# Wide attention products written as four 32-column products, one per column group of TensorE

## The reference

```python
q1 = _split_heads(x @ Wq1, H); q2 = _split_heads(x @ Wq2, H)      # H = 16, head width d = 32
k = _split_heads(x @ Wk, H);   v = _split_heads(x @ Wv, H)
q = jnp.concatenate([q1, q2], axis=1)
k2 = jnp.repeat(k, 2, axis=1); v2 = jnp.repeat(v, 2, axis=1)
scores = jnp.einsum('bhqd,bhkd->bhqk', q, k2) * scale
scores = jnp.where(causal, scores, jnp.finfo(scores.dtype).min)
p = jax.nn.softmax(scores, axis=-1)
y = jnp.einsum('bhqk,bhkd->bhqd', p, v2)
y1, y2 = (y[:, :H], y[:, H:])
y = y1 - lam * y2                                                 # lam = sigmoid(x @ Wlam)
return y.reshape(B, T, D) @ Wo
```

## Time and profile before

| | |
|---|---|
| median of 3 runs | 2073.38 us |
| profiled execution | 2072.73 us |
| its span | 2070.8 us |
| TensorE matmul, share of the span | 96% |
| VectorE, ScalarE, GpSimd | 64%, 40%, 43% |
| mean granted TensorE clock | 0.992 |

### The profile page before, as it was taken

The page is one execution under the profiler, slowest core; times in us unless marked ns, Lnnn a source line. Parts: engine busy times, 40 slices in busy tenths (PEclk is TensorE's granted clock), DMA queues, the critical chain, the costliest instruction groups (busy, mean ns, idle before and its releaser), DMA issues.

```text
span 2070.8 us, 29135 instructions
## 1 busy us (share of the span) xinstructions
PE 1987.4 (96%) x11271; PEld 870.9 (42%) x11312; DVE 1330.7 (64%) x2622; ACT 827.8 (40%) x1259; POOL 880.4 (43%) x459
## 2 busy tenths in 40 slices
PE   7898999899999998999999999999999879899999
PEld 3444444444444444343433434343433324444444
DVE  5868686747847545566666666666667754775644
ACT  4435343425444412344443433344434442543431
POOL 3757575700000000666666667776776670000000
PEclk9999999999999999999999999999999999999999
DMA  7101010120000020000101010010000201000001
GB/s 239 36 26 36 31 36 31 60 94 1 1 0 1 0 57 18 22 16 21 21 22 21 12 28 10 21 22 21 1 22 6 83 10 41 1 0 22 21 1 41
DMA packets 71562, 59.72 MB, mean 29 GB/s; under 512 B 37312, under 2 KB 55744, under 8 KB 71168
## 3 DMA queue, kind: packets, MB, share of 16 engines
q1 hardware_dynamic: 64512, 45.27, 7.6%
q10 hardware_dynamic: 6912, 12.59, 1.9%
HBM read 43.02 MB, written 10.62 MB: 26 GB/s over the span
## 4 chain that ended last, share of the span: by engine, by line
PE 53%; DVE 5%; POOL 2%; ACT 1%; issue 1%; DMA 0%; DVEq 0%; SPq 0%; POOLq 0%; ACTq 0%
PE psum L128 9%; PE psum L1217 9%; PE psum L1308 8%; PE psum L1363 6%; PE psum L1346 6%; PE psum L152 5%; PE psum L1255 3%; PE psum L1342 2%; POOL b_totals L1592 2%; PE psum L1320 2%; PE psum L1265 1%; PE psum L1333 1%; DVE psum L1659 1%; DVE b_maxima L1664 1%; DVE b_down L1722 0%
## 5 line engine op out<-in xcount | busy, mean ns | idle before, releaser
L1592 POOL TENSOR_TENSOR b_totals<-b_totals,b_probs 128x2048 f32<-128x2048 f32 (+5 forms) x160 | 504.4, 3152 | 271.6 <-ACT b_probs L1508 265.8
L1659 DVE CUSTOM_DVE_ANT_0 psum<-psum,b_rest 128x384 f32<-128x384 f32 (+3 forms) x512 | 236.1, 522 | 206.8 <-PE psum L1308 206.6
L1508 ACT ACTIVATE b_probs<-psum 128x1024 f32<-128x1024 f32 (+3 forms) x320 | 228.6, 765 | 244.5 <-PE psum L1346 229.2
L447 PE MATMUL psum<-hT,a_win 128*128 128x512 f32 x640 | 292.5, 600 | 2.6 <-DVE a_parts L751 1.2
L128 PE MATMUL psum<-hT,b_early 128*128 128x512 f16 x1024 | 228.2, 382 | 9.8 <-DVE b_middle L214 6.9
L128 PE MATMUL psum<-hT,W 128*128 128x512 f16 x1024 | 227.4, 382 | 3.7 <-DVE a_win L214 3.6
L1664 DVE TENSOR_REDUCE b_maxima<-psum 128x2 f32<-128x1024 f32 x128 | 150.8, 1220 | 105.9 <-PE psum L1308 105.9
L447 PEld LDWEIGHTS psum<-hT,a_win 128*128 128x128 f32 x640 | 120.2, 192 | 130.5 <-issue 129.2
L128 PEld LDWEIGHTS psum<-hT,b_early 128*128 128x128 bf16 x1024 | 100.1, 98 | 135.2 <-issue 9.7
L128 PEld LDWEIGHTS psum<-hT,W 128*128 128x128 bf16 x1024 | 100.7, 99 | 126.2 <-issue 6.8
L1564 POOL MEMSET b_mask<- 128x128 f32 x1 | 0.2, 204 | 352.2 <-POOLq L279 352.2
(11 more groups left out here) (232 smaller groups left out, 3291.2 us busy)
## 6 DMA issues: line engine op xcount, KB each, us to landing
a_parts<-in_w_guT ACTq DMA_DIRECT2D x32, 256.0 KB, 2.8
ternary<-W SPq DMA_DIRECT2D x1, 6144.0 KB, 18.3
a_win<-in_w_inT SPq DMA_DIRECT2D x20, 256.0 KB, 7.8
a_parts<-in_w_pT ACTq DMA_DIRECT2D x16, 256.0 KB, 2.6
b_down<-lam_rows SPq DMA_DIRECT2D x32, 128.0 KB, 2.6
b_early<-ternary SPq DMA_DIRECT2D x8, 512.0 KB, 8.1
out<-x SPq DMA_DIRECT2D x16, 256.0 KB, 2.2
x<-in_x SPq DMA_DIRECT2D x3, 1024.0 KB, 8.0
```

Source lines behind the costliest of these rows:

```text
L447: last = pe.matmul(ring(s, j), win[:, at:at + P], core["hT"][:, (i * KT + k) * BLK:(i * KT + k + 1) * BLK], start=(k == 0), stop=(k == KT ...
L1508: act.activation(held(u, s)[:, 2 * a:2 * a + 2, off:BLK], pair_banks(("score", u, s, a))[:, :, off:BLK], ACT.Exp, scale=SCALE).then_inc(ex ...
L1592: pool.tensor_tensor(acc, acc, held(u, s)[:, own, off:BLK], ALU.add).then_inc(summed, 1)
L1659: last = dve.tensor_tensor_reduce(scores, scores, row_mask[:, BLK - width:BLK], 1.0, -3e38, ALU.add, ALU.max, maxima[u % 2][:, at:at + 1])
```

## The change

Every product with 128 output partitions in the five places named is written as four products with 32 output partitions each. The four have the same moving operand and each has a quarter of the stationary one; the sums and the place of the results in PSUM stay the same. Semaphore waits stand ahead of the first of the four, and the signal is on the last.

```diff
 HEAD_AT = [0, 2, 1, 3]
+COLUMNS = [slice(j * HD, (j + 1) * HD) for j in range(HPT)]
@@ project (keys, queries)
-                return pe.matmul(to, weights[:, k * P:(k + 1) * P], hT[:, at:at + BLK],
-                                 start=(k == 0), stop=(k == KT - 1))
+                for own in COLUMNS:
+                    last = pe.matmul(to[own, :], weights[:, k * P + own.start:k * P + own.stop], hT[:, at:at + BLK],
+                                     start=(k == 0), stop=(k == KT - 1))
+                return last
@@ fill, values
-                        last = pe.matmul(to[:, t % 2 * 2 * P:(t % 2 + 1) * 2 * P], hT[:, at:at + P],
-                                         wv_all[:, k * D + h * P:k * D + (h + 2) * P],
-                                         start=(k == 0), stop=(k == KT - 1))
+                        for own in COLUMNS:
+                            last = pe.matmul(to[own, t % 2 * 2 * P:(t % 2 + 1) * 2 * P],
+                                             hT[:, at + own.start:at + own.stop],
+                                             wv_all[:, k * D + h * P:k * D + (h + 2) * P],
+                                             start=(k == 0), stop=(k == KT - 1))
@@ output
-                    last = pe.matmul(to[:, j], yT[r % 2][:, t * P:(t + 1) * P], wo_sl[r % 2][:, :],
-                                     start=True, stop=True)
+                    for own in COLUMNS:
+                        last = pe.matmul(to[own, j], yT[r % 2][:, t * P + own.start:t * P + own.stop],
+                                         wo_sl[r % 2][:, :], start=True, stop=True)
@@ scores, mask
-                        pe.matmul(to[j // 2][:, j % 2, off:off + P], ident_b[:, :], later_key[:, :],
-                                  start=True, stop=True)
+                        for own in COLUMNS:
+                            pe.matmul(to[j // 2][own, j % 2, off:off + P], ident_b[:, own], later_key[:, :],
+                                      start=True, stop=True)
```

## The result

The changed kernel takes 2063.03 us (median of 4 runs, 2059.48 to 2063.65) against 2073.40 for the kernel before (4 runs, 2073.01 to 2074.82): a ratio of 0.9946, with a 95% interval from 0.9934 to 0.9958. The forecast was 2062.

The account below looks back on a forecast made before the run. TensorE's own sequence was taken to bound attention. Terms 7.8 + 4.9 + 2.3 − 1.1 − 0.3 − 0.2 − 1.0 − 1.0 = 11.4 us off 2072.73 gave 2061.3, with 0.65 for the median 2062 us; range 2057 to 2084.

Parts of the forecast that it names:

- the issue rival: Issue of four times the instructions becomes TensorE's bound: 2081 us at 33 ns each with half the lookahead; chance 0.16.
- (a): Runs of projections, values or outputs behind another shape, with any mask right behind: 130, each 0.06 cheaper, 7.8 us saved.
- (b): Projection between `weigh` and `row` (steps 0 and 4): 27 places, each 0.18 cheaper, 4.9 us saved.
- (c): `den` (15) or `weigh` (6) right ahead of a mask: a 0.11 change of shape gone, 2.3 us saved.
- the gain goes into waits: Rival: TensorE's gain is lost waiting for the exponential and the maximum in most steps, 2071 us; chance 0.12.
- (d): Behind the still wide `neg` (16 places): 0.16 lost each, counted as 1.1 us for outputs and 0.3 for masks.
- (e): Mask: sixteen narrow bf16 products take what four took; 0.2 us lost where it follows `row` alone.
- (f): Steps 4 and 5: scores wait for the row scores' maximum, so a shorter fill gains nothing; 1.0 us lost.
- (g): Issue of four times the matmul instructions, where a semaphore lets the queue start afresh: 1 us charged.

Follow-up runs that it names:

- e1: The kernel before with only the mask products in 32 columns: 2081.89 us, ratio 1.0040.
- e2: The changed kernel with the mask products wide again, all else narrow: 2072.40 us, ratio 0.9994.
- e3: The kernel before with only the projection between `weigh` and `row` (steps 0 and 4) written in four: 2067.23 us, ratio 0.9972.
- e7: The changed kernel with two products of 64 columns in place of four of 32: 2066.89 us, ratio 0.9967.
- e5: The changed kernel with the last feed-forward layer's up products (f16) in four as well: 2066.55 us, ratio 0.9965.
- e8: The changed kernel with each narrow mask product cut in four along its moving columns, results not the same, read for time alone: 2096.06 us, one run.
- e4: The changed kernel with the output or mask right behind `neg` kept in one wide product: 2064.40 us, ratio 0.9955.

## Why the prediction was right

The theory: what is saved is a gap between groups of different shapes, in which the array is emptied, and the wait for a run's first weights, which is as long as the columns of the load. The rival: four times as many instructions cost issue time. e1 and e2 (parts that don't add), e3 (one join by itself), e7 (a join lost by another width) and e5 (27 ns an instruction held) bear out the first, as far as gap and wait go; that the array is being emptied in the gap is a name for it that no run shows. e8 shows that the issue rival, which lost from 31 ns an instruction on, has no place here.

Point by point, by the starts of all places of a kind before and after:

- (a), 130 runs: forecast 0.06 each, measured 0.060 (a run into scores, 35 places, 0.060; a run into a mask 0.080, less 0.020 for the mask).
- (b), 27 joins with `weigh`: forecast 0.18, measured 0.197 (0.113 ahead of the projection, 0.084 behind); by e3 0.19.
- (c), 21 joins of `den` or `weigh` with a mask: forecast 0.11, measured 0.116. Behind 1578 us, in the last units, it does not last: there TensorE stops in the middle of many masks for ScalarE's exponential, which does not come sooner. The mask that follows `weigh` at 1688.98 us, for instance, waited 1.68 us before its second half, and 1.88 now. What the joins and runs gain in that stretch, about 1.0 us, goes into such waits: the rival "the gain goes into waits", true in this one place.
- (d), behind `neg`: mis-sized. Forecast 0.16 each and 1.4 us in all; the output or mask starts 0.095 later, and e4 shows that none of it reaches the turn. What failed is the step "VectorE's addition too": that the addition ends later because the output does. VectorE isn't waiting for the output there. From the end of `row` on it goes through the maxima, their rounding and that of `neg` without an idle moment, and starts the addition when that is done. In the changed kernel:

```profile
1147.71 0.30 DVE L1666 CUSTOM_DVE_ANT_0 psum<-psum,b_rest 128x128 f32<-128x128 f32 x1 [0.80 <-PE psum L1313]
...
1149.71 0.35 DVE L1705 SCALAR_TENSOR_TENSOR psum<-b_rounded,b_after_part,psum 128x128 f32<-128x128 bf16 x1
1150.10 0.29 DVE L1710 CAST b_negT<-psum 128x128 bf16<-128x128 f32 x1
1150.31 1.21 DVE L1739 TENSOR_TENSOR x<-x,psum 128x1024 f32<-128x1024 f32 x1
```

  And before:

```profile
1155.98 1.21 DVE L1732 TENSOR_TENSOR x<-x,psum 128x1024 f32<-128x1024 f32 x1
```

  The addition starts 2.67 us behind `neg` after and 2.66 before, and `row` 3.94 and 3.93. TensorE's later output ends at about 1149.8, with half a microsecond to spare. The wait in the earlier trace rows named who came last, VectorE, and that was not a sign that VectorE itself waits for the output.
- (e), the mask at no cost: right; 0.01 each where it follows `row` or `den`, 0.2 us in all.
- (f), lost behind VectorE's maxima in steps 4 and 5: forecast 0.06 a unit; `weigh` starts 0.03 to 0.05 later behind the scores in each of the two steps, 0.06 to 0.1 a unit.
- (g), issue: forecast 1.0 us, measured none. e5 and e8 both show room.

With the measured sizes the sum is 7.8 + 5.3 + 2.4 − 0.2 − 1.3 = 14.0 us; the forecast sum was 11.4, and its turn of 110.7 us was measured as 110.63. The traces give 13.0. Taken on the same instructions, TensorE's lead over the kernel before grows steadily from −0.1 us at 777 us to 12.9 at 1578. Behind that it hardly moves, by the waits named under (c), but for 1.5 us around 1638, and these are the granted clock and not the edit. There the kernel before runs at the lower level, 1.2 GHz, for 6.8 us, and the changed kernel for 3.4:

```profile
1638.00:1644.80 6.80, 6.23 (x23) 1.47 (x24) 2.21 (x7) 1.02 (x1) 5.95 (x4) 0.50 0.19 62
```

```profile
1627.50:1630.90 3.40, 3.40 (x19) 1.03 (x12) 0.41 (x1) 0.59 (x1) 3.40 (x2) 0.50 0.36 105
```

The two profiled executions differ by 14.3 us in their spans, through more such things that the edit does not touch. The kernel before has this stretch in an early layer, where the changed kernel has none and comes out 2.8 us sooner:

```profile
405.70:412.50 6.80, 5.61 (x14) 2.02 (x15) 2.13 (x4) 0.63 (x1) 1.43 (x1) 0.50 0.89 231
```

Of that, 1.4 us go into a longer wait for a DMA ahead of the first `row` (2.27 us, 0.89 before), and 1.5 into a stretch of 3.4 us at the lower level from 774 us on. The last layer is 1.4 us shorter at its start, by the clock again, and 1.6 longer here, in the changed kernel:

```profile
1760.50:1764.10 3.60, 3.60 (x11) 1.27 (x9) 0.00 (x0) 0.28 (x1) 0.00 (x0) 0.53 0.00 0
```

Up to the first `neg` the ten profiled kernels take between 815.56 and 818.80 us, though the change leaves that stretch nearly alone. So a whole time carries some 3 us that aren't the edit's.

The medians differ by 10.4 us only. The profiled execution of the changed kernel is the shortest of its four runs, 3.6 us below the median; the spans of the other three are 2060.5 to 2060.8 us, at a mean granted clock of 0.991 where it has 0.993. e4's profiled execution, with the same turn, shows how such a span comes about: 2059.9 us, 11.0 less than before. It has the same 13.0, but is at the lower level for 10.2 us from 815 us on in place of 6.8, which costs 1.3, and waits 1.99 us for the DMA ahead of the first `row`, which costs 1.1. Besides, three of the four executions of the changed kernel have 2.9 to 3.1 us of device time around the span, where the fourth and the kernel before have 1.9; why stays open. The runs that were not profiled have no stretches to read, so that they lost their time as e4 did is likely, not shown.

So the turn and its parts were forecast well, and that the whole time came out within 1 us of the forecast is in part luck: TensorE gained 1.6 us more than the sum, and two to three were lost to the clock, a DMA and the time around the span, which the prediction did not have. Its lowest time does not come out of its own terms either: with nothing lost in (f) and (g) they give 2060, and 2058 only if (d) and (e) cost nothing too.

## What to carry to other kernels

Before narrowing or widening a product, write down the shape (rows by columns of the array) of each group in the order that TensorE takes them, and count the borders: about 0.1 us for each one added or removed, and the first load of a run behind it. Change neighbours together, since a part alone can lose (e1) what the whole gains. And read the gain by the length of a steady loop, not by the whole time, where single microseconds matter.

## What the runs showed of the hardware

- Four f32 products of 32 columns with all rows stream at the same time, and their next weights load behind them: a pass of 512 columns every 0.43 us, as in the wide form. The same holds for bf16 (mask, 0.34 us for sixteen in place of 0.33 for four) and f16 (32 sets of four in 7.02 us with one change of shape in it, where 32 wide ones take 6.91 without one).
- 128 by 32, 128 by 64, 128 by 128 and 32 by 128 count as four different shapes; at each border between two of them that was measured stands a gap of about 0.1 us, between equal ones none, even where the number type changes (f32 `den` to bf16 mask, 0.88 us, two passes).
- TensorE took in 256 instructions in 7.02 us (27 ns each) for one row after the other, and 216 in 3.65 us (17 ns) once a step, and the groups around e8's mask took what they took before. Four abreast with own weights took no less than about 36 ns, at 64 and at 32 moving columns; whether that is issue stays open.
